# Layer with attention and a seven-product feed-forward: partial sums kept in PSUM, sums moved off GpSimd

## The reference, cut to what matters

```python
def attention(q, k, v):                       # 16 heads of 32, keys and values from the context
    return softmax(q @ k.T / sqrt(32)) @ v
x = x + tanh(g_xattn) * linear(attention(rms(layernorm(x) @ wq), rms(ctx @ wk), ctx @ wv), wo)
def ffn(h):                                   # h = layernorm(x), 512 wide
    s = sum(top_2(h @ gate_w))                # one number per token
    y = square(relu(h @ up_w)) @ down_w + (h @ expert_weight) * s    # 2048 hidden units
    return (y - mean(y)) * rsqrt(var(y) + 1e-5) * gamma + beta
x = x + tanh(g_ffn) * ffn(layernorm(x))
```

## Time and profile before

| | |
|---|---|
| median of 3 runs | 1590.77 us (1587.71 to 1596.41) |
| the profiled execution | 1587.87 us, of which the span of the trace 1586.1 us |
| TensorE clock granted, mean | 0.933 of full |
| HBM traffic | 205.08 MB read, 83.10 MB written |

### The profile page before, as it was taken

One profiled execution on the slowest core, in us unless ns is written; L12 is line 12 of the kernel. 1 busy time (PEld: TensorE's weight loads), 2 busy tenths in 40 slices (PEclk: granted clock), 3 DMA queues, 4 the chain that ended last, 5 costly groups with the idle time before them and its releaser, 6 DMA issues.

```text
span 1586.1 us, 26472 instructions
## 1 busy us (share of the span) xinstructions
PE 1319.6 (83%) x9154; PEld 1111.3 (70%) x9154; DVE 1064.7 (67%) x1512; ACT 639.2 (40%) x1888; POOL 969.0 (61%) x977
## 2 busy tenths in 40 slices
PE   7989999999998999779789485879847877989991
PEld 5867777777777777569678365767636866867981
DVE  6776666766687667557768275675645776665795
ACT  6866666766676752124321003431000433112430
POOL 4766666666589648763946464592456476455394
PEclk9998999999999999899999787999869899999996
DMA  6688888888787456677556655546656554555731
GB/s 214 143 226 222 222 205 206 219 207 206 193 201 186 107 173 206 213 180 244 179 167 209 158 164 151 206 154 207 196 136 155 195 171 156 192 191 167 214 106 53
DMA packets 388452, 289.55 MB, mean 183 GB/s; under 512 B 283771, under 2 KB 298235, under 8 KB 383230
## 3 DMA queue, kind: packets, MB, share of 16 engines
q1 hardware_dynamic: 350856, 178.90, 43.0%
q10 hardware_dynamic: 37494, 109.33, 20.4%
HBM read 205.08 MB, written 83.10 MB: 182 GB/s over the span
## 4 chain that ended last, share of the span: by engine, by line
PE 37%; POOL 24%; DVE 12%; issue 9%; DMA 7%; SPq 4%; ACT 3%; ACTq 0%; DVEq 0%; POOLq 0%
PE wide L79 11%; PE wide L80 10%; PE wide L81 10%; DMA pair<-x_scratch 5%; POOL hid L2084 5%; DVE wo_lo L1911 4%; PE wide L418 3%; SPq L1604 2%; PE wide L406 2%; PE wide L427 2%; POOL fxy L2088 2%; POOL hid L2073 2%; DMA out_x<-fxy 1%; POOL pair L2106 1%; POOL hid L2075 1%
## 5 line engine op out<-in xcount | busy, mean ns | idle before, releaser
L1911 DVE TENSOR_TENSOR wo_lo<-hid,wo_hi 128x512 fp32r<-128x512 f32 x224 | 262.3, 1208 | 142.1 <-ACT wo_hi L1771 141.9
L79 PE MATMUL wide<-eight,wo_hi 128*128 128x256 f32 x512 | 152.7, 298 | 63.7 <-DVE wo_lo L1911 55.0
L817 ACT ACTIVATE prob<-wide,nmx 128x128 f32<-128x128 f32 x512 | 182.2, 408 | 35.5 <-DVE nmx L628 35.5
L988 POOL TENSOR_TENSOR prob<-prob,rr 128x512 f32<-128x512 f32 x128 | 132.7, 1049 | 104.3 <-DVE rr L636 102.9
L2084 POOL TENSOR_TENSOR hid<-hid 128x512 f32<-128x512 f32 x96 | 157.8, 1669 | 56.4 <-DVE wo_lo L1911 56.4
L1771 ACT ACTIVATE hid<-wide 128x512 f32<-128x512 f32 x64 | 38.1, 598 | 360.9 <-PE wide L81 360.9
L1771 ACT ACTIVATE wo_hi<-hid 128x512 fp32r<-128x512 f32 x224 | 135.4, 625 | 112.9 <-PE wide L81 112.9
L79 PEld LDWEIGHTS wide<-eight,wo_hi 128*128 128x128 f32 x512 | 99.9, 195 | 74.9 <-issue 48.0
L80 PE MATMUL wide<-eight,wo_hi 128*128 128x256 f32 x512 | 146.8, 287 | 0.0
L81 PE MATMUL wide<-eight,wo_lo 128*128 128x256 f32 x512 | 146.5, 286 | 0.0
L817 ACT ACTIVATION_READ_ACCUMULATOR prob<-wide,nmx 128x1 f32 x512 | 127.4, 249 | 0.0
(11 more groups left out here) (276 smaller groups left out, 4214.6 us busy)
## 6 DMA issues: line engine op xcount, KB each, us to landing
eight<-down_scratch ACTq DMA_DIRECT2D x32, 1024.0 KB, 5.8
xn_scratch<-xs SPq DMA_DIRECT2D x48, 256.0 KB, 5.1
wk_hi<-down_scratch ACTq DMA_DIRECT2D x12, 1024.0 KB, 5.4
wk_lo<-down_scratch ACTq DMA_DIRECT2D x12, 1024.0 KB, 6.1
hid<-xn_scratch SPq DMA_DIRECT2D x48, 256.0 KB, 3.2
wk_hi<-up_scratch ACTq DMA_DIRECT2D x12, 1024.0 KB, 4.8
eight<-up_scratch ACTq DMA_DIRECT2D x12, 1024.0 KB, 7.0
wk_lo<-up_scratch ACTq DMA_DIRECT2D x12, 768.0 KB, 5.7
```

The costliest lines, as they stand in the source:

```text
L79: eng.matmul(dst, ah, bh, start=first and k == 0, stop=False)
L817: i = act.activation(prob[par][:, g, h * P:(h + 1) * P], cols(bank[g], h), ACT.Exp, bias=nmx[:, n:n + 1], scale=1.0, accum_out=rs[:, n:n + 1])
L988: pool.tensor_tensor(p, p, r, ALU.mult).then_inc(po_p, 1)
L1911: dve.tensor_tensor(ff.s_lo[k % KT], hid[q][:, ff.D_SEQ[m][1], :], ff.s_hi[k % KT].bitcast(F32), ALU.subtract).then_inc(ff.dv_l, 1)
```

## The change

What it does, part by part:

1. **Up.** The products of a quarter are summed in PSUM: products 1, 6, 7 and 4 go one onto another in a bank A, 5 and 3 in a bank B, 2 in a bank C; between them ScalarE copies out what the other quarters need. `onto=True` leaves the start flag off. A and B have two banks each, C one. The order of products is `U_ORDER`, in which product 4 of round q runs in round q+1. VectorE has three additions from PSUM a round, one square and one difference; ScalarE has three copies, a relu from PSUM (`relu_21`), and relu and square of the rest in SBUF (`squares`). GpSimd has none.
2. **Between up and down.** VectorE makes the sums S1 and S2 for all rounds in new buffers `S1` and `S24` (`sums_21`), and in down S4 (`sum_4`).
3. **Down.** `D_SEQ` is in a new order, and products 2, 3, 4 and 6 are added onto the contents of their banks, so `collect` is one addition a product, V and GpSimd's additions are gone.
4. **Turning.** `TURN_AT` is spread from slice 9 to 52; ScalarE makes hi two slices after VectorE's transpose, and VectorE, not GpSimd, makes lo three slices after.
5. **Order.** `Y_ORDER` is gone; `result`, `y_stats`, `residual`, `scale_y`, the residual loads and the stores have new places among the rounds; `x_stats`, `x_inv`, `x_normal`, `x_sums`, `deal_x` and `deal_t` of the second half are each one round earlier, `x_sums` of the first half too. In the first group the pieces' splits have new places.
6. **Attention.** The two instructions of `unit_lo_sums` stand after `bias_v` and after `inverse(s, 1)`, no longer ahead of `maxima(s, 0)`.

```diff
@@ attention, VectorE
-                    if ff.second_of(s, par) is not None:
-                        ff.unit_lo_sums(dve, ff.second_of(s, par))
                     maxima(s, 0)
...
                     bias_v(n, 1 - par)
+                    if ff.second_of(s, par) is not None:
+                        ff.unit_lo_sums(dve, ff.second_of(s, par), 0)
                     inverse(s, 1)
+                    if ff.second_of(s, par) is not None:
+                        ff.unit_lo_sums(dve, ff.second_of(s, par), 1)
@@ products and banks
-    U_SEQ = ((0, 0, xa, 0), (0, 1, xa, 2), (0, 3, ta, 2), (0, 2, ta, 0), (1, 1, tb, 0), (1, 0, tb, 2), (1, 2, xb, 2))
-    U_BANK = (4, 5, 6, 7, 1, 0, 2)
-    D_SEQ = ((3, 1), (0, 0), (4, 1), (6, 3), (1, 2), (5, 3), (2, 2))
+    PRODUCT = {1: (0, 0, xa, 0), 2: (0, 1, xa, 2), 3: (1, 2, xb, 2), 4: (1, 0, tb, 2), 5: (0, 2, ta, 0), 6: (0, 3, ta, 2), 7: (1, 1, tb, 0)}
+    A_BANK, B_BANK, C_BANK = (4, 7), (5, 0), 6
+    E_BANK = (1, 2, 0, 5, 4, 6, 7, 5)
+    U_ORDER = [(0, p) for p in (1, 5, 2, 6, 3, 7)]
+    for u in range(1, NQ):
+        U_ORDER += [(u, 1), (u, 5), (u - 1, 4), (u, 6), (u, 2), (u, 3), (u, 7)]
+    U_ORDER.append((NQ - 1, 4))
+    D_SEQ = (0, 3, 4, 2, 5, 1, 6)
@@ upward, TensorE's waits
+        if p == 1:
+            if q > 1:
+                pe.wait_ge(ac_21, n - 1)
...
+        if p == 2 and q > 0:
+            pe.wait_ge(dv_U, 3 * (n - 1) + 1)
+        if p in (6, 3, 7):
+            pe.wait_ge(ac_P, 3 * n + {6: 1, 3: 2, 7: 3}[p])
+        if p == 4:
+            pe.wait_ge(dv_U, 3 * n + 3)
@@ feed_forward
-    TURN_AT = tuple(range(22, 26)) + tuple(range(30, 34)) + tuple(range(38, 42)) + tuple(range(46, 50))
+    TURN_AT = (9, 12, 14, 16, 26, 29, 31, 33, 36, 38, 40, 42, 45, 47, 49, 52)
@@ SyncE
-                    for i in {2: (0,), 3: (1,), 4: (2, 3), 5: (4,), 7: (5,)}.get(q, ()):
+                    for i in {2: (0, 1), 4: (2, 3), 6: (4,)}.get(q, ()):
                         store_out(g - 1, i)
                         load_res(g - 1, i + 2)
...
+                    if q == 6:
+                        deal_x(g + 1, 1)
                     if q == 7:
-                        deal_x(g + 1, 1)
-            if more:
-                deal_t(g + 1, 1)
+                        deal_t(g + 1, 1)
@@ ScalarE
+        def relu_21(g, q):
+            act.wait_ge(ff.pe_P, ff.produced(g, q, 4))
+            act.activation(hid[q][:, 2, :], bank[ff.A_BANK[q % 2]], ACT.Relu).then_inc(ff.ac_21, 1)
+        def squares(g, q):
...
+            act.activation(hid[q][:, 0:2, :], ..., ACT.Relu)     # 128x1024
+            act.activation(hid[q][:, 0:3, :], ..., ACT.Square)   # 128x1536
-                if g < LAST and k in TURN_AT:
-                    ff.hi_T(act, g + 1, TURN_AT.index(k))
+                if g < LAST and k - 2 in TURN_AT:
+                    ff.hi_T(act, g + 1, TURN_AT.index(k - 2))
@@ VectorE
+        def collect(g, m):
+            a, b = ((0, 0), (1, 1), (0, 1), (0, 1), (1, 1), (0, 0), (1, 0))[m]
...
+            dve.tensor_tensor(dst, partial(m), dst, ALU.add).then_inc(ff.dv_D, 1)
+            if g < LAST:
+                if q in (1, 5):
+                    x_stats(g + 1, q // 5)
+                if q in (2, 6):
+                    x_normal(g + 1, q // 6)
...
+                if g < LAST and k - 3 in TURN_AT:
+                    ff.lo_T(dve, g + 1, TURN_AT.index(k - 3))
+                if 2 * NQ + 2 <= k < 3 * NQ + 2:
+                    sum_4(g, k - 2 * NQ - 2)
@@ GpSimd
-            for k in range(NK):
-                if k < NQ:
-                    s234(g, 0, k)
...
-                if g < LAST and k in TURN_AT:
-                    ff.lo_T(pool, g + 1, TURN_AT.index(k))
```

More of the change, by code:

```diff
@@ L71, in flamingo_layer, with mm3 @@
         s_pow = sem("powers_set")
-        def mm3(eng, dst, stat, mov, first=True, last=True, ready=None):
+        def mm3(eng, dst, stat, mov, first=True, last=True, ready=None, onto=False):
             n = len(stat)
@@ L78, in mm3 @@
                     ready(k)
-                eng.matmul(dst, ah, bh, start=first and k == 0, stop=False)
-                eng.matmul(dst, ah, bl, start=False, stop=False)
-                mm = eng.matmul(dst, al, bh, start=False, stop=last and k == n - 1)
+                eng.matmul(dst, ah, bh, start=first and k == 0, stop=False, skip_group_check=onto)
+                eng.matmul(dst, ah, bl, start=False, stop=False, skip_group_check=onto)
+                mm = eng.matmul(dst, al, bh, start=False, stop=last and k == n - 1, skip_group_check=onto)
             return mm
@@ L1494, in lo_T, with product @@
         eng.tensor_tensor(runs(g, t_place(i, 1)), blocks(g, turned(g, i)),
-                          runs(g, t_place(i, 0)).bitcast(F32), ALU.subtract).then_inc(dv_T if g == 0 else po_lT, 1)
-    def product(pe, g, q, n):
-        which, op, (x_hi, x_lo), kk = U_SEQ[n]
+                          runs(g, t_place(i, 0)).bitcast(F32), ALU.subtract).then_inc(dv_T if g == 0 else lo_turned, 1)
+    def product(pe, g, q, p):
+        which, op, (x_hi, x_lo), kk = PRODUCT[p]
         w = chunk_slot(2 * q + which)
@@ new lines, in add_12, with add_22 @@
+        def add_12(g, q):
+            n = g * NQ + q
+            dve.wait_ge(ff.pe_P, ff.produced(g, q, 3))
+            dve.wait_ge(ff.ac_P, 3 * n + 3)
+            dve.tensor_tensor(hid[q][:, 1, :], bank[ff.B_BANK[q % 2]], hid[q][:, 1, :], ALU.add).then_inc(ff.dv_U, 1)
+        def add_22(g, q):
+            n = g * NQ + q
+            dve.wait_ge(ff.pe_P, ff.produced(g, q, 7))
+            dve.wait_ge(ff.ac_P, 3 * n + 2)
+            dve.tensor_tensor(hid[q][:, 3, :], bank[ff.A_BANK[q % 2]], hid[q][:, 3, :], ALU.add).then_inc(ff.dv_U, 1)
@@ L1883, in sum_3 @@
[L1883 to L1896 removed]
+            if q == 0:
+                dve.wait_ge(ff.pe_P, NK * (g + 1))
@@ L1987, in x_normal, with y_centre @@
                 ff.normalise(dve, g, jj + HB)
+        def y_centre(g, i):
+            y_stats(g, i)
+            centre(g, i)
         def fill_a(g, q):
-            if g > 0 and q == 0:
-                y_stats(g - 1, 0)
-                centre(g - 1, 0)
-                y_stats(g - 1, 1)
-                centre(g - 1, 1)
+            if g > 0:
+                for i in {2: (0, 1), 6: (4,)}.get(q, ()):
+                    result(g - 1, i)
             if q == 5:
@@ L2022, in fill_b @@
             if g == 0 and q == 0:
                 prepare()
-            if more:
-                if q == 1:
-                    x_stats(g + 1, 0)
-                if q == 2:
-                    x_normal(g + 1, 0)
-                if q == 6:
-                    x_stats(g + 1, 1)
-                if q == 7:
-                    x_normal(g + 1, 1)
+            if g > 0:
+                for i in {4: (2, 3)}.get(q, ()):
+                    result(g - 1, i)
+                for i in {0: (0, 1), 3: (2, 3), 4: (4,), 7: (5, 6)}.get(q, ()):
+                    y_centre(g - 1, i)
@@ L2042, in group @@
-                sum_3(g, q)
-                fill_b(g, q)
-            finish(g, NQ - 1)
+                    add_22(g, q - 1)
+                    square_22(g, q - 1)
+                if lo:
+                    ff.piece_lo_a(dve, q + 1, 0)
+                else:
+                    fill_b(g, q)
+                if lo:
+                    ff.piece_lo_a(dve, q + 1, 1)
+                    fill_b(g, q)
+                if q > 1:
+                    sum_3(g, q - 2)
+                fill_a(g, q)
@@ L2045, in group @@
+                add_11(g, q)
+                add_12(g, q)
+            add_22(g, NQ - 1)
+            square_22(g, NQ - 1)
+            sum_3(g, NQ - 2)
             if g > 0:
-                y_stats(g - 1, 7)
-                centre(g - 1, 7)
+                result(g - 1, 5)
                 result(g - 1, 6)
-                result(g - 1, 7)
+                y_centre(g - 1, 7)
+            sum_3(g, NQ - 1)
+            for q in range(NQ):
+                sums_21(g, q)
+                if q == HB and g > 0:
+                    result(g - 1, 7)
```

535 lines of the change are left out of this document (230 added, 305 removed).

## The result

The changed kernel takes 1452.53 us (median of 4 runs, 1447.07 to 1455.89) against 1591.36 for the kernel before (1587.71 to 1596.41): ratio 0.9122, 95% interval 0.9084 to 0.916. The forecast was 1403, its range 1365 to 1475. So the direction and the range held, and of the 188 us forecast as gain some 139 came. The profiled execution has a span of 1453.8 us against 1586.1.

The account below looks back on a forecast made before the run. Bound: TensorE's list of matmuls plus the waits inside it. Gains of 42 (attention), 86 (down), 42 (up) and 18 (experts) sum to 188; 1587.9 profiled becomes 1400, plus 2.9 for the median gives 1403 us, range 1365 to 1475.

Parts of the forecast that it names:

- Down, 86 forecast: Down stages: 82.5 us a group, 416.3 falling to 330, so 86 us gained; bounds 92 and 36.
- that rival: Down: VectorE becomes the bound, down costs 95 to 100 us in three groups, whole 1440 to 1455; chance 0.14.
- Up, 42 forecast: Up stages: gains of 10.6, 15.2, 9.7 and 6.2 us over four groups, 42 us together; bounds 65 and 0.
- The stall at `x_stats`: Up, second and third group: VectorE waits for `load_x` until 77 us, holding up product 4; an 18 us stall.
- The sentence that residuals no longer stop TensorE: Up: loads of residuals 2 and 3 go ahead of the deals, `result` follows a round or more later; no separate size.
- The bound of 65 for "no stall": Up: the better bound of the gain, 65 us instead of 42, if no stall occurs.
- Attention, 42 forecast: Attention unit slots: moving `unit_lo_sums` behind `bias_v` gains 4.2 us at each of ten waits, 42 us; bounds 50 and 29.
- the sentence that let 0.8 us through: Attention: of the moved instructions' 2.1 us and later transfers, 0.8 us a slot is lost from the 5.0 us gain.
- The last rival, that the wait only moves along: Attention: the change does less than it says, the wait moving along its slot; whole 1445, chance within another rival's 0.12.
- Experts, 18 less forecast: Expert stages: 38.2 and 38 to 30 us, first 32.3 to 30, last 25.1 to 25.5; 18 us gained, bounds 28 and 0.
- tile 7's result, at 16: Experts: tile 7's result at 16 us, landing at about 24, frees the last product's bank; down starts at 30.
- The rival that small waits pull it down: Up: small waits in each round lower the clock, costing 44 us and as much in waits; about 1490, chance 0.04.

Follow-up runs that it names:

- experiment 5: Changed kernel, but GpSimd again subtracts the high part of the next group's turned tokens (lo), as in the kernel before: 1452.4 us, ratio 0.9143.
- experiment 4: Changed kernel with unit transfers split (high parts stored, next unit loaded earlier) and both `unit_lo_sums` back ahead of the maxima: 1465.24 us, ratio 0.9205.
- experiment 7: Changed kernel, three SyncE orders: second-half loads before sums' deals, 1457.19 us; store 5 and load 7 before last deals, 1453.83; second half one round later, 1441.55.

## Why the prediction was right, and where it was not

The range held because its upper end had room for the rivals; the forecast itself is 50 us off.

- **Down, 86 forecast, 92 measured.** Right in size, and in what the stage looks like: TensorE's slices at 1.44 us without a gap, VectorE's lo at a median of 0.69 us. VectorE is busy for 65 us where 75 were summed, since instructions of 0.69 us that follow each other start 0.60 apart. Which cause did it is argued and not shown: experiment 5 puts the share of lo_T at zero, and some 50 of the 92 us go with the groups that turn tiles. VectorE did not become the bound, so that rival fell.
- **Up, 42 forecast, 42 measured, in part by luck.** The stall at `x_stats` came in the second and third group, at 74 us for 77, and cost TensorE 11.5 and 10.7 us where 18 were forecast: product 4 was ready at 69 us and not at 64. The sentence that residuals no longer stop TensorE is wrong, for the 3.0 us at 54 us into the stage stand behind one; the 3 us forecast at `x_normal` did not reach TensorE (VectorE waits 2.75 there). The half clock cost 4.6 us (busy for 85.4 against 80.8 in the last up) where 2 were put. These cancel in part: 99.8 and 99.3 for 104, 9 us more gained than forecast. The first group gave nothing (109.5 for 101), 8.5 us less than forecast. What sets its pace was not taken apart; the forecast named the weights' pieces, but with plain deals alone it is 6.5 us shorter (108.2 for 114.7 to the experts' first product). The last is 80.8 for 80.5. The bound of 65 for "no stall" does not follow from its terms either: without the 23.5 us in two groups the sum gives 89.
- **Attention, 42 forecast, 8.7 measured in one execution, 11 in medians, 16 to 19 in five other executions with the same attention code.** The step that failed is the sentence that let 0.8 us through and its lower bound of 29. The loss of 5.0 us a slot was real (experiment 4: 49 us in ten pairs), and the new place does remove it. What I missed is that the next slot's tile is stored behind the unit's 2.25 MB, that this chain was short by about 2 us once the slot was shorter, and that a miss there costs TensorE's idle time and the half clock again. The prediction named late transfers but gave them no price. The last rival, that the wait only moves along, is for the greater part what happened.
- **Experts, 18 less forecast, 11.6 more measured.** Two steps failed, by about the same amount. One is "tile 7's result, at 16". SyncE was done with issuing the deals 15 to 16.5 us into the stage (13 forecast), but the residual of tile 7 is loaded behind store 5, which is issued behind the deals; the result came at 30. I counted the stores behind the deals and not the load. The other is a term put at nothing: the waits for the experts' weights, 5.2, 4.0, 3.4 and 2.3 us, 15 in all. Before, only the first group had such a wait (8.7 us) and the last one of 0.9.
- **The clock.** The rival that small waits pull it down fell: the last up, on the same shared banks, has 1.00. In the changed kernel's trace every stretch of half clock among the matmuls stands behind one wait of TensorE, the shortest 1.9 us at the very start and 2.3 after it, the others 2.4 to 11.5. The page TensorE: Matmul & The Clock Gate of the Trainium skill, section A second HAM failure mode: psum-queue depth-cycling, warns of such oscillation; no run here shows it.

Left open: what the banks, the moved sums and the new places of the turns each give in down, since they were not taken apart; what makes the experts' weights late; and GpSimd's `x_inv` ahead of its residual, which experiment 7 points to and which was not tried.

## What to carry to other kernels

A wait that is taken out of a slot is gained only up to the next chain that ends there or in the slot behind it: before pricing it, follow every transfer due in the following slot and ask by how much it was early. Two waits in series on one period have to be removed together, and then each looks worthless alone (0 and 11 us) while both give 48 (1463.71 less 1416.03). For an in-order queue, write down what each load stands behind, not only each store; and where transfers of short runs fill the queue, their layout can be worth more than any order of them: 52 us here, in a kernel that leaves out the rearrangement and so only bounds the gain, against some 10 for the orders tried.

## What had not been expected of the hardware

- Issuing is not free for the engine that does it: four transfers cost ScalarE 3.7 us of its time at each unit, and SyncE's issue of one 256 KB load stood 4.75 us behind the unit's 2.25 MB.
- 256 KB in runs of 128 bytes kept SyncE 3.8 us each (8 in 30.6 us) beside the loads of weights, and the same bytes in whole rows 2.3 us (8 in 18.3 us).
- Storing a part of the bunch earlier let the next small store land 1.2 us sooner (6.1 for 7.3), and a pair of slots took 4 us less.
- The same attention code took 553 to 563 us in six profiled executions, in which the slots behind the units took anything from 15.4 to 22.3 us; with the bunch split it took 522 to 525 in four.
